# Adjacency loaded as 64 tiles of 4 MB into two buffers instead of 128 halves of 2 MB into four

## The chip, the core and the metric

The kernel runs on one core of a Trainium2 chip. The metric is the device time of one execution in microseconds (us). It works with five engines (TensorE for matmuls, VectorE, ScalarE, GpSimd, and SyncE, which only issues transfers) and with the core's 16 DMA engines. In the profile they are called PE (its weight loads PEld), DVE, ACT, POOL and SP.

## What is computed

One layer of graph attention over a sparse adjacency matrix. `x` is 8192 x 128 float32; `adj` is 8192 x 8192 int32, with a one in some 4 of the 8192 places of a row; `attn` is 256 x 1.

```python
h = jnp.maximum(_layernorm(x, axis=-1), 0.0)
s_i = h @ attn[:d]
s_j = h @ attn[d:]
e = jax.nn.leaky_relu(s_i + s_j.T, negative_slope=0.2)
e = e + jnp.where(adj > 0, jnp.float32(0.0), neg_inf)
alpha = jax.nn.softmax(e, axis=1)
return x + alpha @ h
```

The 256 MB of `adj` have to be read once; everything else is small beside them.

## The kernel before

**Tiles.** The 8192 rows are cut into 64 tiles of 128 rows (row `64 * p + t` stands in partition p of tile t). Two tiles are a pair. A tile of the adjacency is 128 partitions with 8192 int32 each, 32 KB in a row and 4 MB in all. The kernel handles it in two halves of 4096 columns; half n is half n % 2 of tile n // 2.

**The loads.** `adj_ring` holds four halves (64 KB in each partition). SP issues all loads, in `load_pair(p)`: the four halves of pair p, each as one transfer (line 356) of 2 MB, 16 KB from each of 128 rows, into slot `n % 4`. Each slot has its own semaphore `adj_in[s]`. The first four are issued at once. From then on the load of half n waits until half n - 4 has been signed (`signed`, line 355), so that up to four halves are under way or waiting to be used. After the loads of pair p, SP issues the store of pair p - 4 of the output (128 KB, line 361).

**The stages behind a load.** ACT turns a half into signs (`sign_tile`, line 533, int32 to bf16, with the row's sum as a by-product) and counts `signed`. PE packs the eight chunks of a tile's signs into one number per column (`pack_tile`, lines 1152 and 1160: four or eight matmuls as soon as a half is signed) and counts `packed`. DVE finds the columns with ones by maxima over these numbers (`max_tile`, `find_pair`, `flag_pair`, `key_pair`). POOL fetches the neighbours' rows of h by indirect DMA from a table in HBM (`gather_pair`, line 455, twelve gathers for a pair; rows of crowded lists by line 470). DVE scores them (`score_pair`), ACT takes the exponential (`exp_pair`, between the two halves of a pair's first tile), and DVE adds them up (`add_pair`, line 797).

**The start.** ACT's own order is fixed by hand: the layer norm of x by quarters (`root_quarter`, `relu_quarter`, line 544, 16 activations for a quarter) and, between them, `sign_tile(0)` behind `relu_quarter(1)` and `sign_tile(1)` behind `relu_quarter(2)`. The scored rows of h are stored to the table in four transfers of 1 MB, issued by POOL (line 441), and the first gather waits for all of them.

**The end.** When the last tile is through, DVE does the parts that need all rows (`lone_mark` and what follows), and the last lists and the last two pairs are mixed.

The order on every engine is the order of the code; no scheduler moves anything.

Of the kernel before, what the change touches and what calls it, by code (L numbers as in the profile page):

```python
# [5 lines left out]
def graph_attention_kernel(nc: bass.Bass, x: bass.AP, adj: bass.AP, attn: bass.AP, out: bass.AP):  # L6
# [10 lines left out]
    HALF = N // 2  # L17
# [52 lines left out]
    adj_t = adj.rearrange("(p t) c -> t p c", p=P)  # L70
# [3 lines left out]
    with ctx:  # L74
        def sb(name, shape, dt):
            return ctx.enter_context(nc.sbuf_tensor(name, shape, dt))
# [4 lines left out]
        def sem(name):  # L81
            return ctx.enter_context(nc.semaphore(name))

        adj_ring = sb("adj_ring", [P, 4, HALF], i32)
# [151 lines left out]

        x_in = [sem(f"x_in{i}") for i in range(XC)]
        attn_in = sem("attn_in")
        adj_in = [sem(f"adj_in{i}") for i in range(4)]
        consts = sem("consts")  # L240
        near_zeroed = sem("near_zeroed")
        ones_ready = sem("ones_ready")
# [17 lines left out]
        signed = sem("signed")  # L260
# [83 lines left out]
        @block.sync  # L344
        def _(sp):
            for c in range(XC):
                sp.dma_start(x_all[:, c * XT:(c + 1) * XT, :], x_t[:, c * XT:(c + 1) * XT, :]).then_inc(x_in[c], 16)
                if c == 0:
                    sp.dma_start(attn_b[:, :], attn.rearrange("d o -> o d").broadcast_to([P, 2 * D])) \
                        .then_inc(attn_in, 16)  # L350

            def load_pair(p):
                for s in range(4):
                    if p > 0:
                        sp.wait_ge(signed, 4 * p + s - 3)
                    sp.dma_start(adj_ring[:, s, :], adj_t[2 * p + s // 2, :, (s % 2) * HALF:(s % 2 + 1) * HALF]) \
                        .then_inc(adj_in[s], 16)

            def store_pair(g):
                sp.wait_ge(pair_mixed, g + 1)  # L360
                sp.dma_start(out_t[:, 2 * g:2 * g + 2, :], mixed[:, g % 2, :, :]).then_inc(stored[g % 2], 16)

            load_pair(0)
            load_pair(1)
            for p in range(2, PAIRS):
                load_pair(p)
                for g in MIXES.get(p - 2, []):
                    store_pair(g)
            for g in range(PAIRS - 4, PAIRS):
                store_pair(g)  # L370

            sp.wait_ge(sizes_ready, 2)
            tiles = sp.value_load(far_tiles[0:1, 0:1], min_val=1, max_val=TILES)
            parts = sp.value_load(far_parts[0:1, 0:1], min_val=1, max_val=DC)
            with sp.Fori(0, tiles) as t:
                with sp.Fori(0, parts) as c:
                    sp.wait_ge(far_used, DC * t + c + 1)
                    sp.sem_inc(sp_passed, 1)
                    sp.dma_start(far_h, table[ds(c * DW + 1, DW), :].rearrange("(k q) c -> q k c", q=P)) \
                        .then_inc(far_h_in, 16)  # L380
                    sp.dma_start(far_adj, adj_t[ds(t, 1), :, ds(c * DW, DW)].rearrange("o p w -> (o p) w")) \
                        .then_inc(far_adj_in, 16)
# [140 lines left out]
        @block.scalar  # L523
        def _(act):
            act.wait_ge(consts, 1)

            def sign_tile(t, halves=(0, 1)):
                for h in halves:
                    n = 2 * t + h
                    act.wait_ge(adj_in[n % 4], 16 * (n // 4) + 16)  # L530
                    if n >= 4:
                        act.wait_ge(packed, n - 3)
                    nc.scalar.activation(sign_ring[:, n % 4, :], adj_ring[:, n % 4, :], ACT.Sign, bias=half_neg[:, :],  # L533
                                         accum_out=degree[:, t, h:h + 1]).then_inc(signed, 1)

            def root_quarter(c):
                cs = slice(c * XT, (c + 1) * XT)
                act.wait_ge(setup, 8 * c + 8)
                nc.scalar.activation(rstd[:, cs], var[:, cs], ACT.Sqrt).then_inc(std_ready, 1)

            def relu_quarter(c):
                act.wait_ge(scaled, 2 * c + 2)
                for t in range(c * XT, (c + 1) * XT):
                    nc.scalar.activation(h_all[:, t, 0:D], x_all[:, t, :], ACT.Relu,  # L544
                                         bias=shift[:, t:t + 1], scale=rstd[:, t:t + 1]).then_inc(h_ready, 1)

            def exp_pair(g):
                act.wait_ge(below_ready, g + 1)
                nc.scalar.activation(weight[:, g % 2, :], below[:, g % 2, :], ACT.Exp).then_inc(weight_ready, 1)

            def exp_m(m):
                act.wait_ge(below_m_ready, m + 1)
                nc.scalar.activation(weight_m[:, :], below_m[:, :], ACT.Exp, accum_out=total_m[:, :]) \
                    .then_inc(weight_m_ready, 1)

            root_quarter(0)
            root_quarter(1)
            relu_quarter(0)
            root_quarter(2)
            root_quarter(3)  # L560
            relu_quarter(1)
            sign_tile(0)
            relu_quarter(2)
            sign_tile(1)
            def exp_step(p):
                for g in MIXES.get(p, []):
                    exp_pair(g)
                m = p // SEG - 1
                if m >= 0 and p % SEG == DEEP_MIX:
                    exp_m(m)  # L570

            for p in range(1, PAIRS):
                sign_tile(2 * p, (0,))
                exp_step(p - 1)
                sign_tile(2 * p, (1,))
                sign_tile(2 * p + 1)
            exp_step(PAIRS - 1)
            for c in range(LC):
                part = lone_p[:, c * LT * P:(c + 1) * LT * P]
                act.wait_ge(lone_masked, c + 1)  # L580
                nc.scalar.activation(part, part, ACT.Exp).then_inc(lone_exp, 1)  # L581
            exp_pair(PAIRS - 2)
            exp_pair(PAIRS - 1)
            exp_m(SEGS - 1)

            act.wait_ge(sizes_ready, 2)
            tiles = act.value_load(far_tiles[0:1, 0:1], min_val=1, max_val=TILES)
            parts = act.value_load(far_parts[0:1, 0:1], min_val=1, max_val=DC)
            with act.Fori(0, tiles) as t:
                with act.Fori(0, parts) as c:  # L590
                    act.wait_ge(far_neg_ready, DC * t + c + 1)
                    act.sem_inc(act_passed, 1)
                    nc.scalar.activation(far_p, far_masked, ACT.Exp, bias=far_neg[:, :]).then_inc(far_exp, 1)
                    nc.scalar.activation(far_scale[:, :], far_old[:, :], ACT.Exp, bias=far_neg[:, :]) \
                        .then_inc(far_exp, 1)
                    act.wait_ge(far_turned, DC * t + c + 1)
                    act.sem_inc(act_passed, 1)
                    nc.scalar.activation(far_pt, far_u, ACT.Copy).then_inc(far_pt_ready, 1)
# [687 lines left out]
```

## Time and profile before

| | us |
|---|---|
| median of 3 runs | 868.03 |
| lowest, highest | 866.7, 868.43 |
| the profiled execution, its own time | 867.93 |
| its span (first to last record) | 866.2 |

So 1.7 us of the profiled execution lie outside its span, and it is 0.1 us from the median. Busy times of the span: DVE 66%, POOL 66%, ACT 60%, PE 53%. "DMA share" is the mean busy share of the 16 DMA engines. A time in a view counts from the span's start. A wait in the views names what came last before the engine went on; a transfer's "to landing" is from its issue on SP or POOL to the semaphore that tells its end.

### The profile page before, as it was taken

How to read it: one execution, taken by the hardware profiler on the slowest of the kernel's cores; microseconds unless marked ns; L12 is line 12 of the kernel's file. 1: busy time of each engine (PE TensorE's matmuls, PEld its weight loads, DVE VectorE, ACT ScalarE, POOL GpSimd, SP SyncE). 2: the span in 40 equal slices, each digit the busy share in tenths (PEclk: the TensorE clock that was granted, in tenths of full speed). 3: DMA queues.
4: the chain of work that ended last, by engine and by line, in shares of the span. 5: the costliest groups of instructions: out<-in, count | busy, mean ns of one | idle time of the engine just before them, and what ended most of it. 6: DMA issues, size and time to landing. Idle time of an engine off the chain costs nothing.

```text
span 866.2 us, 7055 instructions
## 1 busy us (share of the span) xinstructions
PE 460.1 (53%) x1605; PEld 191.2 (22%) x1633; DVE 569.3 (66%) x2273; ACT 521.1 (60%) x357; POOL 571.0 (66%) x527
## 2 busy tenths in 40 slices
PE   0665465655555665566555656556566455623601
PEld 0332122221212222122222222222222122213600
DVE  7998266565676666656766465568656566668981
ACT  1895676666676666676666666667666677600200
POOL 6631776666567777666678777667776867758810
PEclk9998777676886678776788686876767788665955
DMA  8799999999999999999999999999999999511000
GB/s 346 286 382 404 399 406 409 410 410 410 406 408 409 410 408 409 405 410 411 404 406 410 408 411 406 414 405 412 404 405 403 408 391 404 196 25 27 18 16 14
DMA packets 39515, 301.56 MB, mean 348 GB/s; under 512 B 10611, under 2 KB 16948, under 8 KB 22065
## 3 DMA queue, kind: packets, MB, share of 16 engines
q1 hardware_dynamic: 24176, 277.23, 79.1%
q0 software_dynamic: 15296, 23.88, 8.0%
q8 instruction: 13, 0.21, 0.1%
q14 instruction: 30, 0.24, 0.1%
HBM read 303.63 MB, written 8.91 MB: 361 GB/s over the span
## 4 chain that ended last, share of the span: by engine, by line
DMA 69%; issue 13%; DVE 11%; ACT 5%; PE 1%; DVEq 0%; POOL 0%; SPq 0%; ACTq 0%; POOLq 0%
DMA adj_ring<-in_adj_dram 68%; ACT sign_ring L533 3%; DVE mixed L797 1%; DVE one_hot L609 1%; ACT h_all L544 1%; DVE adj_ring L954 1%; DVE adj_ring L958 1%; DVE adj_ring L949 1%; DVE mixed_m L879 1%; DMA x_all<-in_x_dram 1%; PE words L1160 0%; DVE codes L616 0%; DVE codes L619 0%; PE words L1220 0%; PE words L1223 0%
## 5 line engine op out<-in xcount | busy, mean ns | idle before, releaser
L533 ACT ACTIVATE sign_ring<-adj_ring,half_neg 128x4096 bf16<-128x4096 int32 x128 | 474.6, 3708 | 226.4 <-DMA adj_ring<-in_adj_dram 226.4
L455 POOL DMA_INDIRECT near<-h_table,near_id x384 | 443.8, 1156 | 198.9 <-issue 109.2
L1160 PE MATMUL words<-sign_ring,pack_w 128*128 128x512 bf16 x1004 | 357.2, 516 | 282.3 <-ACT sign_ring L533 279.6
L656 DVE MAX8 cand<-words 128x8 f32<-128x256 f32 x256 | 91.1, 418 | 223.9 <-PE words L1160 223.8
L1160 PEld LDWEIGHTS words<-sign_ring,pack_w 128*128 128x128 bf16 x1024 | 114.1, 121 | 516.7 <-ACT sign_ring L533 357.2
L797 DVE SCALAR_TENSOR_TENSOR mixed<-near,weight_n,mixed 128x128 f32<-128x128 f32 x448 | 120.3, 345 | 0.0
L470 POOL DMA_INDIRECT near_m<-h_table,id_m x64 | 79.1, 1235 | 19.5 <-issue 19.5
L1152 PE MATMUL words<-place,place_w 128*128 128x512 bf16 x120 | 47.2, 478 | 1.1 <-issue 1.0
L1142 PE MATMUL listing<-h_all 128*1 128x128 f32 x128 | 20.4, 335 | 33.7 <-ACT h_all L544 33.7
L581 ACT ACTIVATE adj_ring<-adj_ring 128x2048 f32<-128x2048 f32 x4 | 7.6, 1910 | 49.8 <-DVE adj_ring L958 49.8
L1179 PEld LDWEIGHTS listing<-cand,one_hot 128*128 128x128 f32 x128 | 28.1, 271 | 12.6 <-issue 6.5
L1229 PE MATMUL words<-h_all,adj_ring 128*128 128x129 f32 x128 | 18.8, 316 | 15.7 <-ACT adj_ring L581 15.7
L1179 PE MATMUL listing<-cand,one_hot 128*128 128x34 f32 x128 | 23.3, 317 | 2.5 <-DVE one_hot L745 2.5
L533 ACT ACTIVATION_READ_ACCUMULATOR sign_ring<-adj_ring,half_neg 128x1 f32 x128 | 23.9, 186 | 0.0
L434 POOL TENSOR_SCALAR h_all<-x_all,codes 128x128 f32<-128x128 f32 x16 | 13.0, 825 | 14.5 <-DVE codes L628 14.5
L1142 PEld LDWEIGHTS listing<-h_all 128*1 128x1 f32 x128 | 12.8, 102 | 41.4 <-issue 27.1
L672 DVE TENSOR_TENSOR codes<-cand_i,code_mask 128x512 int32<-128x512 int32 x32 | 21.9, 684 | 0.0
L1229 PEld LDWEIGHTS words<-h_all,adj_ring 128*128 128x128 f32 x128 | 18.1, 229 | 16.4 <-ACT adj_ring L581 16.4
L642 DVE TENSOR_TENSOR near<-h_all,mixed 128x2048 f32<-128x2048 f32 x8 | 21.5, 2683 | 0.0
L797 DVE SCALAR_TENSOR_TENSOR mixed<-near,weight_n,x_all 128x128 f32<-128x128 f32 x64 | 19.8, 350 | 1.1
L544 ACT ACTIVATE h_all<-x_all,codes 128x128 f32<-128x128 f32 x48 | 18.8, 480 | 0.2 <-DVE codes L628 0.2
L647 DVE TENSOR_REDUCE h_all<-near 128x16 f32<-128x2048 f32 x8 | 18.3, 2288 | 0.3
(213 smaller groups left out, 431.4 us busy)
## 6 DMA issues: line engine op xcount, KB each, us to landing
adj_ring<-in_adj_dram SPq DMA_DIRECT2D x128, 2048.0 KB, 18.9
near<-h_table,near_id POOLq DMA_INDIRECT x384, 6.4
h_table<-h_all POOLq DMA_DIRECT2D x4, 1056.0 KB, 12.2
x_all<-in_x_dram SPq DMA_DIRECT2D x4, 1024.0 KB, 9.6
out_dram<-mixed SPq DMA_DIRECT2D x32, 128.0 KB, 18.5
near_m<-h_table,id_m POOLq DMA_INDIRECT x64, 6.2
adj_ring<-h_table SPq DMA_DIRECT2D x1, 132.0 KB, 3.1
mixed<-in_L_gnn_attn_dram SPq DMA_DIRECT2D x1, 128.0 KB, 6.5
```

Of the source, the lines that this page charges most:

```text
L455: pool.indirect_dma_start(out=near[:, p % RING, k, :], out_offset=None, in_=table, in_offset=bass.IndirectOffsetOnAxis(ap=near_id[:, p % I ...
L470: pool.indirect_dma_start(out=near_m[:, k, :], out_offset=None, in_=table, in_offset=bass.IndirectOffsetOnAxis(ap=id_m[:, k:k + 1], axis=0 ...
L533: nc.scalar.activation(sign_ring[:, n % 4, :], adj_ring[:, n % 4, :], ACT.Sign, bias=half_neg[:, :], accum_out=degree[:, t, h:h + 1]).then ...
L544: nc.scalar.activation(h_all[:, t, 0:D], x_all[:, t, :], ACT.Relu, bias=shift[:, t:t + 1], scale=rstd[:, t:t + 1]).then_inc(h_ready, 1)
L656: last = nc.vector.max(out=cand[:, p % 2, t % 2, 8 * q:8 * q + 8], in_=words[t % 3][:, q * PART:(q + 1) * PART])
L672: nc.vector.tensor_tensor(codes[:, :, :, :].rearrange("p a w c -> p (a w) c"), cand_i[:, :, :].rearrange("p a w -> p (a w)").unsqueeze(2). ...
L797: ins = nc.vector.scalar_tensor_tensor(acc, near[:, e, slot, 0:D], weight_n[:, a * own + k:a * own + k + 1], base, ALU.mult, ALU.add)
L1142: last = nc.tensor.matmul(listing[0:1, 0:D], h_all[:, t, ONE:ONE + 1], h_all[:, t, 0:D], start=(t == 0), stop=(t == TILES - 1))
L1152: nc.tensor.matmul(at[:, k * BANK:(k + 1) * BANK], place_w[:, :], place[:, k * BANK:(k + 1) * BANK], start=True, stop=False)
L1160: last = nc.tensor.matmul(at[:, k * BANK:(k + 1) * BANK], pack_w[:, c, :], sign_ring[:, n % 4, o + k * BANK:o + (k + 1) * BANK], start=Fal ...
L1179: last = nc.tensor.matmul(listing[:, 0:REC], one_hot[:, p % 2, a, :], cand[:, p % 2, a, :], start=(p % SEG == 0 and a == 0), stop=(p % SEG ...
L1229: last = nc.tensor.matmul(lone_sum, lone_p[:, t * P:(t + 1) * P], h_all[:, t, 0:ONE + 1], start=(t == 0), stop=(t == TILES - 1))
```

## The change

A load brings a whole tile, in one transfer of 128 rows with 32 KB each, into two neighbouring slots. There are two semaphores, one for each half of the ring. The load of tile t waits until both halves of tile t - 2 have been signed. ACT waits for its tile's semaphore ahead of either half. The memory used, the signs, their ring of four halves and all else stay.

```diff
-        adj_in = [sem(f"adj_in{i}") for i in range(4)]
+        adj_in = [sem(f"adj_in{i}") for i in range(2)]
...
             def load_pair(p):
-                for s in range(4):
+                for e in range(2):
                     if p > 0:
-                        sp.wait_ge(signed, 4 * p + s - 3)
-                    sp.dma_start(adj_ring[:, s, :], adj_t[2 * p + s // 2, :, (s % 2) * HALF:(s % 2 + 1) * HALF]) \
-                        .then_inc(adj_in[s], 16)
+                        sp.wait_ge(signed, 4 * p + 2 * e - 2)
+                    sp.dma_start(adj_ring[:, 2 * e:2 * e + 2, :].rearrange("p h c -> p (h c)"), adj_t[2 * p + e, :, :]) \
+                        .then_inc(adj_in[e], 16)
...
                     n = 2 * t + h
-                    act.wait_ge(adj_in[n % 4], 16 * (n // 4) + 16)
+                    act.wait_ge(adj_in[t % 2], 16 * (t // 2) + 16)
```

On SP, from the loads of x to the second store, the order before is:

```order
L347 DMA x_all<-in_x_dram 128x2048 x3
L356 DMA adj_ring<-in_adj_dram 128x4096 x4
L356 DMA adj_ring<-in_adj_dram 128x4096 [waits signed] x16
L361 DMA out_dram<-mixed 128x256 [waits pair_mixed]
L356 DMA adj_ring<-in_adj_dram 128x4096 [waits signed] x4
L361 DMA out_dram<-mixed 128x256 [waits pair_mixed]
```

and now, at the same place:

```order
L347 DMA x_all<-in_x_dram 128x2048 x3
L356 DMA adj_ring<-in_adj_dram 128x8192 x2
L356 DMA adj_ring<-in_adj_dram 128x8192 [waits signed] x8
L361 DMA out_dram<-mixed 128x256 [waits pair_mixed]
L356 DMA adj_ring<-in_adj_dram 128x8192 [waits signed] x2
L361 DMA out_dram<-mixed 128x256 [waits pair_mixed]
```

Nothing has moved past another instruction; each two loads have become one of twice the width, and the stores stand between the same tiles. On ACT the place is the two signs of tile 0, the quarter of the layer norm behind them, and tile 1; each half waited for a semaphore of its own, and now both halves of a tile wait for the same one:

```order
-L533 ACTIVATE sign_ring,degree<-adj_ring,half_neg 128x4096 [waits adj_in0]
-L533 ACTIVATE sign_ring,degree<-adj_ring,half_neg 128x4096 [waits adj_in1]
+L533 ACTIVATE sign_ring,degree<-adj_ring,half_neg 128x4096 [waits adj_in0] x2
 L544 ACTIVATE h_all<-x_all,codes 128x128 [waits scaled]
 L544 ACTIVATE h_all<-x_all,codes 128x128 x15
-L533 ACTIVATE sign_ring,degree<-adj_ring,half_neg 128x4096 [waits adj_in2]
-L533 ACTIVATE sign_ring,degree<-adj_ring,half_neg 128x4096 [waits adj_in3]
```

The order of ACT's instructions is the same as before; only what they wait for differs. PE, DVE and POOL have the same instructions and waits.

## Rows read from the trace of the kernel before

**Rows 1.** Page, parts 1 and 2: busy time, share and instructions; DMA packets by size.

```profile
PE 460.1 (53%) x1605; PEld 191.2 (22%) x1633; DVE 569.3 (66%) x2273; ACT 521.1 (60%) x357; POOL 571.0 (66%) x527
...
DMA packets 39515, 301.56 MB, mean 348 GB/s; under 512 B 10611, under 2 KB 16948, under 8 KB 22065
```

**Rows 2.** Chain that ended last, in order of time: start us, us, what.

```profile
101.33 0.19 ACT sign_ring L533
101.54 18.81 DMA adj_ring<-in_adj_dram
120.40 3.59 issue
...
736.15 0.19 ACT sign_ring L533
```

**Rows 3.** Waits of the whole span: who for whom: us, times, longest.

```profile
PE words L1160 <- ACT sign_ring L533: 279.6, 118, 4.7
ACT sign_ring L533 <- DMA adj_ring<-in_adj_dram: 226.4, 122, 4.1
DVE cand L656 <- PE words L1160: 223.8, 46, 9.2
```

**Rows 4.** Busy time by stretch; the last three: PEclk, DMA share, GB/s.

```profile
10.00:20.00 10.00, 0.00 (x0) 0.00 (x0) 9.78 (x29) 1.52 (x3) 5.63 (x23) 1.00 1.02 431
...
36.00:41.00 5.00, 4.97 (x32) 3.18 (x32) 4.97 (x3) 5.00 (x3) 5.00 (x7) 0.70 0.11 29
41.00:52.00 11.00, 6.62 (x30) 3.08 (x31) 10.93 (x5) 11.00 (x19) 8.63 (x7) 0.87 0.99 380
52.00:66.00 14.00, 10.01 (x70) 5.84 (x68) 13.90 (x7) 13.64 (x9) 0.76 (x2) 0.98 0.99 375
66.00:88.00 22.00, 12.53 (x53) 5.52 (x55) 18.57 (x74) 12.37 (x7) 4.28 (x6) 0.84 0.99 407
...
110.00:736.00 626.00, 362.60 (x1138) 133.76 (x1159) 394.88 (x1765) 424.00 (x252) 445.25 (x388) 0.75 1.01 407
```

**Rows 5.** Timeline of ACT at the start: start us, us, what.

```profile
35.60 3.69 ACT L533 ACTIVATE sign_ring<-adj_ring,half_neg 128x4096 bf16<-128x4096 int32 x1
...
39.29 3.70 ACT L533 ACTIVATE sign_ring<-adj_ring,half_neg 128x4096 bf16<-128x4096 int32 x1
```

**Rows 6.** Tile adj_ring, 39.3 to 39.5 us: the load issued there.

```profile
L356 SPq DMA_DIRECT2D adj_ring<-in_adj_dram x1: 327/327/327, 39.4 to 39.4; - x1
...
DMA to landing us min/median/max: 8.0/8.0/8.0
```

**Rows 7.** DMA issues: transfer, queue, count, KB each, median us to landing.

```profile
adj_ring<-in_adj_dram SPq DMA_DIRECT2D x128, 2048.0 KB, 18.9
near<-h_table,near_id POOLq DMA_INDIRECT x384, 6.4
...
adj_ring<-h_table SPq DMA_DIRECT2D x1, 132.0 KB, 3.1
```

**Rows 8.** Timeline of ACT, 403 to 440 us: the second half of four tiles.

```profile
403.34 3.71 ACT L533 ACTIVATE sign_ring<-adj_ring,half_neg 128x4096 bf16<-128x4096 int32 x1 [1.60 <-DMA adj_ring<-in_adj_dram]
...
414.05 3.71 ACT L533 ACTIVATE sign_ring<-adj_ring,half_neg 128x4096 bf16<-128x4096 int32 x1 [1.46 <-DMA adj_ring<-in_adj_dram]
...
425.81 3.71 ACT L533 ACTIVATE sign_ring<-adj_ring,half_neg 128x4096 bf16<-128x4096 int32 x1 [1.77 <-DMA adj_ring<-in_adj_dram]
...
437.48 3.71 ACT L533 ACTIVATE sign_ring<-adj_ring,half_neg 128x4096 bf16<-128x4096 int32 x1 [2.86 <-DMA adj_ring<-in_adj_dram]
```

**Rows 9.** Page, part 3: DMA queues: packets, MB, share of 16 engines.

```profile
q1 hardware_dynamic: 24176, 277.23, 79.1%
q0 software_dynamic: 15296, 23.88, 8.0%
```

**Rows 10.** Chain that ended last, from the last load's issue on.

```profile
755.26 3.81 ACT sign_ring L533 x2
...
759.12 3.57 PE words L1160 x8
```

## Prediction

> **What bounds the kernel now.** I read the page's chain of waits first, because every engine is only 53 to 66% busy [rows 1], so busy time alone names no bound. The chain is loads of the adjacency for most of the span, and in order of time it is one pattern, repeated [rows 2]: ACT finishes a half, SP issues the next load into that slot, the load lands 18.8 us later, ACT signs (3.6 us as "issue" and 0.2 us), and so on. A turn of this pattern is four halves, one pair. Between its first and last piece shown there are 28 turns in 736.15 - 101.33 = 634.8 us, so a pair takes 22.67 us, a tile 11.34, a half 5.67. The table of waits says who is late in there: PE waits for ACT, DVE for PE, ACT for the loads, 122 times [rows 3]. ACT needs 3.9 us for a half and gets one every 5.67, so the compute side has room. The stretches say why the loads are late: from 110 to 736 us the DMA engines are busy all the time, at 407 GB/s [rows 4]. So the middle is bound by the DMA engines' work, not by the time from issue to landing. The 18.9 us of a load [rows 7] are mostly queueing: at its issue nearly three other halves (3 x 5.67 = 17 us) stand ahead of it.
>
> The question for the change is therefore not what a transfer costs, but whether the engines still always have work. A larger transfer in the same memory gives the same bytes, with a slot that comes free later and data that can be used later.
>
> **Part 1, the start: +3.7 us.** The ring is full before ACT is ready to sign: from 36 to 41 us the DMA engines are at 0.11 of their time [rows 4]. The first half is signed from 35.60 to 39.29 and the second to 42.99 [rows 5]. The fifth load is issued at 39.4 [rows 6]; its successor, the load of tile 2, must wait for both halves, to about 43.1. The hole grows by one sign, 3.7 us. What would hide this is a later hole in the same stretch, which could shrink. There is none: the shares of the stretches from 41 to 88 us are 0.98 to 0.99 [rows 4], work of loads and table stores together. Tile 3 is issued as its second half was before. So the whole stream moves by 3.7 us. Bounds: 0 (if a hole later on takes it up) and 3.7; I take 3.7, because the stretches show no such hole.
>
> **Part 2, the end: +3.7 us.** Of the last tile, the first half is already signed when the second lands. Then come one sign, 3.81 us with its accumulator read, and one group of 8 matmuls, 3.57 us [rows 10]. Afterwards the tile lands as a whole and ACT signs two halves, 2 x 3.7. PE packs the first of them beside the second sign, 3.57 us under 3.7, so only one sign more lies on the path. DVE waits for that and everything behind it moves. Bounds 3.6 and 3.9.
>
> **Part 3, the middle: +2.5 us, uncertain.** Here the depth decides. Let a tile land at T. Before, the slot of half n was free 3.8 us after landing, with three halves ahead of the new load. Now both halves are signed at T + 7.4, with 0.2 for the exponential in between on every other tile and 0.1 to the issue: T + 7.6 to 7.7. The only work left for the slowest DMA engine is tile t + 1, due to land at T + 11.34. For the stream not to pause, the fixed part of a load (issue to first byte, and last byte to semaphore) has to fit into 11.34 - 7.65 = 3.7 us. One load of the trace was issued into an empty queue and tells this part: 8.0 us from issue to landing [rows 6], of which 2.10 MB at the 431 GB/s of the stretch from 10 to 20 us are 4.9 us (an estimate; at the middle's 407 it would be 5.15) [rows 4], so 3.1 fixed. The 132 KB load at the end takes 3.1 in all [rows 7]. These two agree although one is 16 times larger, so I take 3.1 for 4 MB also. Room on average: 0.6 us.
>
> Tiles are not even, though. The starts of the second halves in the timeline are 10.7, 11.8 and 11.7 us apart [rows 8]. I carried this rule through the 56 tiles whose second halves start between 120.4 [rows 2] and 755.3 us [rows 10] (56 distances, mean 11.34): each tile takes its own distance on the stream, and starts when the one ahead is through or 3.1 us less the landing part after its issue, whichever is later. The pauses add up to 2.5 us with 3.1 fixed, 0.1 with 2.6, 5 with 3.3, 10 with 3.6, 22 with 4.2 and 41 with 4.9. I take 2.5.
>
> In the trace the gathers, which are tiny, land 6.4 us after issue [rows 7] under full load, twice the 3.1 of the lone small load. Part of that is POOL's own issuing and part waiting behind load packets, but some can be slower access under load, which a fixed part read from an idle machine does not have. The Trainium skill, "DMA: Bandwidth & Descriptors", section on latency and other measured facts, speaks against this change here: HBM access takes 0.2 us on average and 2 us at high load, and it is the main component of the fixed cost. By that rule up to 1.8 us would come on top; the rows neither show nor exclude it.
>
> **Part 4, fewer packets: -3.2 us.** A row of 16 KB is one packet now: 128 x 128 = 16384 of the 24176 packets of q1 [rows 9], near the 39515 - 22065 = 17450 packets of 8 KB and more [rows 1]. With 32 KB rows there are 8192 fewer, if the queue does not split them. What does a packet cost beside its bytes? Two queues give two equations [rows 9]. q1 took 0.791 x 16 x 866.2 = 10963 us of engine time for 24176 packets and 277.23 MB; q0 took 0.080 x 16 x 866.2 = 1109 us for 15296 packets and 23.88 MB. Solved, a packet costs 12.5 ns. 8192 x 12.5 ns / 16 engines = 6.4 us. The packets of the two queues are of different kinds, so this is a rough estimate; 0 (rows split back, or no such cost) and 6.4 are the bounds, and I take the middle, since neither queue has only such packets.
>
> **What is free.** SP issues 64 instructions fewer, 0.33 us each [rows 6], in time it spends waiting. `signed`, `packed` and the ring of signs are untouched; a sign in the second tile on needs a half packed four halves ago, 22.67 us of stream earlier. PE gets its halves in bursts of two, 2 x 4 us of matmuls in 11.34. The exponential's input comes from DVE one pair ahead. Table stores share the engines with packets twice as long, so they may end some us later; DVE then gets its first gathers later, but ACT needs what PE packed four halves earlier, so the stages behind ACT can slip by some us without reaching a load. If this cover were gone, the start would cost those few us more.
>
> **Sum.** 867.93 (the profiled execution's own time) + 3.7 + 3.7 + 2.5 - 3.2 = 874.6. The profiled execution is 0.1 from the median 868.03, so the median of after should be **874.7**, 0.8% slower.
>
> **Rivals.**
>
> *A. The queue runs dry for every tile.* Same mechanism as part 3, but the fixed part of a 4 MB load issued under load is 3.6 to 4.9 us. For it: the 6.4 us of the gathers, and the rule above. Against it: 2 MB and 132 KB have the same fixed part. It decides from about 3.3 us on. Time: 872.2 (the sum without its 2.5) + 10 to 41 = 882 to 913; with 4.2, 894. Signs: ACT's wait for the load would start to follow SP's issue, and the DMA share of the middle would fall to 0.97 or less.
>
> *B. No change.* The ends cost 7.4, packets give the full 6.4, and the fixed part is near 2.6: 867.93 + 7.4 + 0.1 - 6.4 = 869.0. For it: the equations of part 4. Against it: all three must fall its way.
>
> *C. Faster.* The stream has room: it moves 407 GB/s in the middle while the stretch from 10 to 20 us reached 431 [rows 4]. If longer packets alone raised the rate by 2%, 0.02 x 635 = 12.7 us, the time would be 867.93 + 7.4 + 2.5 - 12.7 = 865.1. It decides from 10 us of gain on, a rate 1.6% higher. The Trainium skill, same page, section on bandwidth, has a rule that would give more: 341 GB/s for 1 MB transfers and 425 for 16 MB. This holds for transfers measured one by one; the rows of the middle show no idle time between transfers for a larger one to remove. Against C: the bytes and the engines' time for a byte are unchanged, and the gathers take their share as before.
>
> *D. The rows are split into 16 KB again.* Then part 4 is zero: 877.8, inside the forecast's own range.
>
> **How the numbers follow.** Forecast (with D) 0.58, from 870 to 881: ends 7.4, middle 0 to 8, packets 0 to -6.4. A 0.25, from 881 to 913. B 0.12, C 0.05. A measurement here can tell about 0.2%, 1.7 us: below 866.3 is faster, up to 869.8 the same. That gives faster 0.05, same 0.12, slower 0.83. The range of 868.5 to 894 leaves out C, a little of B, and the upper part of A.
>
> **What would show it.** The fifth load's counterpart issued near 43 us and a hole in the DMA share some 3.7 us longer: part 1. Two signs and one pack behind the last landing: part 2. The distance of tiles in the middle: 11.34 plus 0.04 for part 3, less 0.06 for part 4; over 11.5 would be A, under 11.2 C. q1 with about 16,000 packets instead of 24,176 would show the longer rows. The prediction is wrong above all if the fixed part of a large load under load is not 3.1 us.

## The result, and the profile after

The changed kernel takes 887.8 us (median of 4 runs, 884.3 to 890.2) against 867.4 beside it. The ratio is 1.023 with a 95% interval of 1.019 to 1.027, so it is 2.3% slower. The profiled execution took 889.62 us with a span of 887.9, that is 21.7 more than the profiled one before. The ratios below leave out executions more than 1.5% above the fastest of their kernel (one of 1858 us, of the kernel with halves first, among them), and the traces of the kernel with the first scoring later and of the one freed by halves and used by tiles are of such executions, so their waits, rates and delays at a tile are read and not their totals.

I predicted 874.7 and gave 868.5 to 894: the sign was right and the size was inside the range, but the loss of 20.4 us is three times the 6.7 I called likeliest. The surprise is where the time went. First the page's parts 1 to 3 and 6, to compare with [rows 1], [rows 7] and [rows 9]:

```profile
span 887.9 us, 6991 instructions
...
DMA packets 30298, 301.56 MB, mean 340 GB/s; under 512 B 9586, under 2 KB 15923, under 8 KB 21040
...
q1 hardware_dynamic: 14960, 277.23, 78.0%
q0 software_dynamic: 15296, 23.88, 8.2%
...
adj_ring<-in_adj_dram SPq DMA_DIRECT2D x64, 4096.0 KB, 15.1
...
h_table<-h_all POOLq DMA_DIRECT2D x4, 1056.0 KB, 24.5
```

The rows of 32 KB travel as one packet each: q1 has 9216 packets fewer, the 8192 of the rows and 1024 that belong to the 64 transfers saved. The 1 MB stores of the table, which the change doesn't touch, land after 24.5 us (median); before:

```profile
h_table<-h_all POOLq DMA_DIRECT2D x4, 1056.0 KB, 12.2
```

The stretches of after (the last three columns are PEclk, DMA share, GB/s), to compare with [rows 4]:

```profile
36.00:41.00 5.00, 5.00 (x32) 3.08 (x31) 4.96 (x3) 5.00 (x3) 5.00 (x7) 0.66 0.00 0
41.00:52.00 11.00, 6.61 (x35) 3.38 (x36) 10.93 (x5) 11.00 (x19) 8.63 (x7) 0.92 0.68 268
...
110.00:736.00 626.00, 344.16 (x1116) 124.26 (x1137) 387.07 (x1723) 410.58 (x250) 446.71 (x392) 0.76 0.99 395
...
118.00:128.00 10.00, 0.00 (x0) 0.00 (x0) 1.22 (x8) 2.01 (x3) 7.80 (x8) 0.52 0.74 288
128.00:136.00 8.00, 7.12 (x27) 3.23 (x29) 7.35 (x36) 7.97 (x6) 6.14 (x7) 0.74 0.50 146
```

The first hole is longer, as expected: (1 - 0.68) x 11 + 5 = 8.5 us against 0.89 x 5 + 0.01 x 11 = 4.6 before, so 3.9. But there is a second one between 118 and 136 us that I had not forecast: 0.26 x 10 + 0.50 x 8 = 6.6 us of the DMA engines' time. The chain of waits of after shows its cause, in order of time:

```profile
70.34 32.29 DMA h_table<-mixed
...
118.07 8.55 DMA near<-h_table,near_id
...
126.64 0.23 DVE score L753
...
128.03 0.02 ACT weight L549
```

Loads are no longer on the chain there. The last store of the table lands after 32 us, the twelve gathers of pair 0 can start only then, DVE waits for them to score pair 0, and ACT waits for DVE to take the exponential between the two signs of tile 6. The two traces' tables of waits, after and then before:

```profile
POOL near L455 <- DMA h_table<-mixed: 32.7, 1, 32.7
DVE score L753 <- DMA near<-h_table,near_id: 27.8, 5, 22.5
...
ACT weight L549 <- DVE below L769: 18.4, 3, 8.0
```

```profile
POOL near L455 <- DMA h_table<-mixed: 13.0, 1, 13.0
```

ACT's timeline at tile 6, before and after. The table load in it is for the exponential's function:

```profile
107.30 1.28 ACT L549 ACT_TABLE_LOAD   x1
108.59 0.22 ACT L549 ACTIVATE weight<-below 128x16 f32<-128x16 f32 x1
109.16 3.71 ACT L533 ACTIVATE sign_ring<-adj_ring,half_neg 128x4096 bf16<-128x4096 int32 x1 [0.35 <-DMA adj_ring<-in_adj_dram]
...
131.74 3.71 ACT L533 ACTIVATE sign_ring<-adj_ring,half_neg 128x4096 bf16<-128x4096 int32 x1 [1.63 <-DMA adj_ring<-in_adj_dram]
```

```profile
114.92 3.71 ACT L533 ACTIVATE sign_ring<-adj_ring,half_neg 128x4096 bf16<-128x4096 int32 x1 [3.50 <-DMA adj_ring<-in_adj_dram]
...
118.74 1.28 ACT L549 ACT_TABLE_LOAD   x1
128.03 0.21 ACT L549 ACTIVATE weight<-below 128x16 f32<-128x16 f32 x1 [8.00 <-DVE below L769]
128.15 3.69 ACT L533 ACTIVATE sign_ring<-adj_ring,half_neg 128x4096 bf16<-128x4096 int32 x1
...
146.04 3.71 ACT L533 ACTIVATE sign_ring<-adj_ring,half_neg 128x4096 bf16<-128x4096 int32 x1 [6.71 <-DMA adj_ring<-in_adj_dram]
```

A tile is complete when its second half starts before the change and its first half after it. That gives the account of the 21.7 us:

| | before | after | late by |
|---|---|---|---|
| tile 6 complete | 109.16 | 114.92 | 5.8 |
| tile 8 complete | 131.74 | 146.04 | 14.3 |
| tile 63 complete | 755.26 | 775.32 | 20.1 |
| end of span | 866.2 | 887.9 | 21.7 |

So 14.3 us are lost in the first 146 us, of which 8.5 between tiles 6 and 8 (of the 5.8 up to tile 6, the longer hole explains 3.9; the rest was not traced), 5.8 us in the 55 tiles of the middle, and 1.6 behind the last landing.

### The profile page after: what moved, and what is told of

It is laid out like the page before. It is cut to its first block, busy times and chain, and to the rows that moved or that the text cites. A ratio compares the mean times of both kernels' runs of the same rounds, so it can differ in the third digit from the quotient of the medians.

```text
span 887.9 us, 6991 instructions
## 1 busy us (share of the span) xinstructions
PE 446.1 (50%) x1605; PEld 182.5 (21%) x1633; DVE 570.9 (64%) x2273; ACT 514.5 (58%) x357; POOL 567.6 (64%) x527
## 3 DMA queue, kind: packets, MB, share of 16 engines
q1 hardware_dynamic: 14960, 277.23, 78.0%
## 4 chain that ended last, share of the span: by engine, by line
DMA 54%; issue 15%; DVE 14%; ACT 13%; POOL 1%; PE 1%; DVEq 0%; SPq 0%; ACTq 0%; POOLq 0%
DMA adj_ring<-in_adj_dram 49%; ACT sign_ring L533 13%; DMA h_table<-mixed 4%; DVE near L642 2%; DVE mixed L797 1%; DVE one_hot L609 1%; POOL near L455 1%; DVE adj_ring L954 1%; DVE adj_ring L958 1%; DVE adj_ring L949 1%; DMA near<-h_table,near_id 1%; DVE mixed_m L879 1%; DVE h_all L647 1%; DMA x_all<-in_x_dram 1%; DVE codes L616 0%
## 5 line engine op out<-in xcount | busy, mean ns | idle before, releaser
L1152 PE MATMUL words<-place,place_w 128*128 128x512 bf16 x120 | 37.7, 390 | 0.9 <-issue 0.7
L1179 PE MATMUL listing<-cand,one_hot 128*128 128x34 f32 x128 | 19.9, 284 | 19.2 <-DVE one_hot L745 19.2
L1179 PEld LDWEIGHTS listing<-cand,one_hot 128*128 128x128 f32 x128 | 22.3, 221 | 25.6 <-DVE one_hot L745 20.3
L753 DVE TENSOR_SCALAR score<-near,h_all 128x8 f32<-128x8 f32 x32 | 7.6, 237 | 28.0 <-DMA near<-h_table,near_id 27.8
## 6 DMA issues: line engine op xcount, KB each, us to landing
adj_ring<-in_adj_dram SPq DMA_DIRECT2D x64, 4096.0 KB, 15.1
h_table<-h_all POOLq DMA_DIRECT2D x4, 1056.0 KB, 24.5
out_dram<-mixed SPq DMA_DIRECT2D x32, 128.0 KB
mixed<-in_L_gnn_attn_dram SPq DMA_DIRECT2D x1, 128.0 KB, 6.3
```

The lines of the kernel that those rows point to most:

```text
L1152: nc.tensor.matmul(at[:, k * BANK:(k + 1) * BANK], place_w[:, :], place[:, k * BANK:(k + 1) * BANK], start=True, stop=False)
L1179: last = nc.tensor.matmul(listing[:, 0:REC], one_hot[:, p % 2, a, :], cand[:, p % 2, a, :], start=(p % SEG == 0 and a == 0), stop=(p % SEG ...
```

## Experiments

The kernel before took 882 and 880 us (medians) in the two sessions of the first eight runs and 866 in that of the last four. So only ratios to the kernel before of the same session are compared between sessions, and traces by stretches. Starts at tile 0 differ by 2.8 us in some traces; delays at a tile are taken from ACT's first sign.

The kernel before was not traced in the first two sessions, and their traces differ from the others in two ways that don't follow the form of the loads. Behind 330 us the rate falls even in kernels with a fine ring, as the lines further down show. And from the last tile's completion to the end of the span they take 110 to 128 us, where the traces of the other sessions take 110 to 113. So the stretch from 160 to 330 us is what I compare, and a difference of some us between two totals of these sessions is not put down to a stage.

**Whole tiles by two transfers: are the long packets the cause?**

```diff
-                    sp.dma_start(adj_ring[:, 2 * e:2 * e + 2, :].rearrange("p h c -> p (h c)"), adj_t[2 * p + e, :, :]) \
-                        .then_inc(adj_in[e], 16)
+                    for h in range(2):
+                        sp.dma_start(adj_ring[:, 2 * e + h, :], adj_t[2 * p + e, :, h * HALF:(h + 1) * HALF]) \
+                            .then_inc(adj_in[e], 16)
...
-                    act.wait_ge(adj_in[t % 2], 16 * (t // 2) + 16)
+                    act.wait_ge(adj_in[t % 2], 32 * (t // 2) + 32)
```

> The changed kernel, but each tile comes by two transfers of 2 MB (16 KB rows) that are issued together once the whole tile is free; ACT still waits for the whole tile. Only the length of a packet differs from the changed kernel. Theory P (32 KB packets take the DMA engines from the table's stores, whose packets are 8 KB; the table is late by 20 us, DVE waits 22.5 us for the first gather, ACT 8 us for its exponential): the last part of the table lands 13 to 15 us after its issue instead of 32.3, DVE's wait for the gathers is near 12, no stall of ACT, and the time is 887.8 - 8 = 877 to 880. Theory D (the late table comes from the stream as a whole being late or from the slots that free late, not from the packets): table wait and time stay as in the changed kernel, 886 to 890.

Measured: 1.028 (1.021 to 1.035) times before. Its table of waits and two stretches, the second around the issue of a tile's two loads at 201 us:

```profile
POOL near L456 <- DMA h_table<-mixed: 14.1, 1, 14.1
```

```profile
160.00:330.00 170.00, 90.07 (x288) 31.81 (x294) 99.38 (x447) 107.43 (x64) 102.57 (x96) 0.74 1.00 383
```

```profile
202.00:204.00 2.00, 1.95 (x11) 1.04 (x10) 0.68 (x2) 0.00 (x0) 0.00 (x0) 1.00 0.85 279
```

With 16 KB rows the table is on time again (14.1 us instead of 32.7), ACT is held up 1.5 us at tile 6 instead of 9.5, and tile 8 is 5.0 us late instead of 14.3. Theory P holds for the start. Its time was a miss: the total did not fall, because the middle is slower here, 383 GB/s between 160 and 330 us. From tile 8 to tile 63 this kernel loses 28 us, where the changed kernel loses 5.8. Neither theory had that. I come back to it below.

**The first scoring one pair later: does ACT's stall cost what it lasts?**

```diff
-        MIXES = {p: [p - 2] for p in range(2, PAIRS)}
+        MIXES = {p: [p - 2] if p > 3 else [0, 1] for p in range(3, PAIRS)}
```

> The changed kernel with the first pair scored one pair later (pairs 0 and 1 are both mixed in turn 3), so that DVE doesn't wait for the first gather in turn 2. Loads and packets as in the changed kernel. Theory P and D both say that the table stays late (32 us). If the stall of ACT behind DVE's wait is what costs (tile 8 starts 14.3 us late, tile 6 only 5.8), the time falls by about 8 to 879 to 881. If that stall would have been made up later by the stream, the time stays at 886 to 890.

Measured: 1.023 (1.013 to 1.033). The table stayed late (POOL waited 30.5 us). Tile 8 was now only 3.7 us late, about what the first hole gives, so what the changed kernel loses beyond it up to tile 8 hangs on the stall. But the stall had only moved: ACT waited at tile 8, for the exponential of pair 1. POOL issues a gather every 1.3 us, so 24 gathers for two pairs take 31 us from 102 us on, and one pair's respite is too little:

```profile
139.51 1.28 ACT L549 ACT_TABLE_LOAD   x1
140.81 0.21 ACT L549 ACTIVATE weight<-below 128x16 f32<-128x16 f32 x1
148.22 0.22 ACT L549 ACTIVATE weight<-below 128x16 f32<-128x16 f32 x1 [7.20 <-issue]
```

My expected 8 us of gain was a miss; the experiment shows the mechanism up to tile 8, not a remedy. Its executions scatter widely, from 892.6 to 906.3 us.

**Halves at the start, tiles later, and the reverse: how much belongs to which stretch?** `load_pair` and `sign_tile` follow the old form for some pairs and the new one for the rest, with semaphores of their own:

```diff
+                    if p < 5:       # the reverse kernel: p >= 5
+                        for h in range(2):
+                            if p > 0:
+                                sp.wait_ge(signed, 4 * p + 2 * e + h - 3)
+                            sp.dma_start(adj_ring[:, 2 * e + h, :], adj_t[2 * p + e, :, h * HALF:(h + 1) * HALF]) \
+                                .then_inc(half_in[2 * e + h], 16)
+                        continue
...
```

> Pairs 0 to 4 by halves as before the change, pairs 5 to 31 by whole tiles. If the start holds most of the loss, as the two traces say (14.3 of 21.7 us by tile 8, 5.7 from there to tile 63, 1.6 behind), the time is that of before + 6 to 9: 873 to 877. If the loss lies in every tile of the middle (fixed part of a load above 3.6 us), it is 884 to 890.

> The other way round: pairs 0 to 4 by whole tiles, the rest by halves. If the start holds most of the loss: before + 13 to 15, 880 to 883. If the middle holds it: 869 to 872 (only the 3.7 of the start).

Measured: 1.012 (1.002 to 1.022) with halves first, 1.022 (1.016 to 1.028) with tiles first. In the traces, tile 8 is 0.0 us late with halves first and 13.1 with tiles first. From 160 to 330 us the first moves 399 GB/s and the second 409, what the kernel before has. So the loss up to tile 8 belongs to the way the first pairs are loaded (row length and grain together), and the lower rate from 160 to 330 us to the way the later ones are. The time with halves first lies in its expected range (6 to 9 us is 0.7 to 1.0%); that with tiles first, 2.2%, is above the 13 to 15 us expected, and its stretches behind 330 us move only 398 and 391 GB/s, although they are loaded by halves. The two losses add to more than the changed kernel's, but the intervals are wide.

**The changed kernel again, in the same session.**

> The changed kernel once more, beside the experiments on the same chip, since the kernel before ran at 882 us in the chip session of the first experiments and at 867 beside the first runs. Both theories: 1.8 to 2.8% over the kernel before; the table's last part lands 30 us or more after its issue.

Measured: 1.018 (1.013 to 1.024); POOL waited 30.6 us for the table.

**Which coarseness costs in the middle: freeing or using?** One kernel frees by tiles and uses by halves (the load's wait before the halves 0 and 2 of a pair only); the other frees by halves and uses by tiles.

```diff
-                    if p > 0:
-                        sp.wait_ge(signed, 4 * p + s - 3)
+                    if p > 0 and s % 2 == 0:
+                        sp.wait_ge(signed, 4 * p + s - 2)
```

> Transfers of 2 MB with 16 KB rows, issued in twos once a whole tile is free, but ACT signs a half as soon as that half lands. Theory G (in the middle the cost comes from the coarse grain: slot free 7.6 us after the tile lands): signing begins 5 us before the tile is complete, so the slots free some 3.7 us earlier than in the changed kernel, the queue never dries, and the middle is as before; with the start's 3.7 us the time is that of before + 3 to 5 us (0.4 to 0.6%). Theory Q (two loads issued together cost something of their own, as in the kernel of two loads for a tile, which was no faster than the changed one): 2% or more over before.

```diff
-                    act.wait_ge(adj_in[n % 4], 16 * (n // 4) + 16)
+                    for both in (2 * t, 2 * t + 1):
+                        act.wait_ge(adj_in[both % 4], 16 * (both // 4) + 16)
```

> Loads exactly as before the change, each issued when its half slot is free, but ACT waits for both halves of a tile. A slot frees 5.67 us later for the first half, 0 to 3.7 later for the second. Theory G: the load of the first half of tile t + 2 is issued at T + 3.8 with 7.5 us of stream ahead of it, so the middle stays as before; the start too, since ACT is the later there; the end costs one sign. Time: before + 3 to 5 us. If grain of use alone were the cost: 1.5% or more over before.

Measured: 1.011 (1.005 to 1.016) and 1.002 (0.998 to 1.006). The stretches of the two, in this order:

```profile
160.00:330.00 170.00, 100.04 (x314) 36.33 (x314) 105.43 (x471) 114.82 (x68) 112.75 (x99) 0.75 1.01 410
...
330.00:500.00 170.00, 102.26 (x308) 36.73 (x308) 105.26 (x467) 111.50 (x68) 117.69 (x104) 0.71 1.00 392
500.00:736.00 236.00, 135.85 (x428) 49.59 (x428) 152.16 (x669) 158.69 (x97) 161.94 (x146) 0.71 1.00 398
```

```profile
160.00:330.00 170.00, 99.28 (x317) 35.33 (x316) 104.54 (x465) 113.59 (x68) 113.96 (x102) 0.75 1.01 409
...
330.00:500.00 170.00, 98.83 (x313) 35.06 (x311) 107.89 (x481) 110.22 (x68) 117.11 (x104) 0.74 1.00 398
500.00:736.00 236.00, 126.60 (x434) 46.54 (x435) 144.94 (x636) 156.51 (x97) 154.63 (x141) 0.77 0.99 393
```

and the first of them in the changed kernel:

```profile
160.00:330.00 170.00, 97.71 (x309) 35.06 (x316) 102.67 (x461) 112.24 (x68) 114.31 (x102) 0.75 1.00 404
```

Between 160 and 330 us either coarseness alone keeps the rate of before, 409 GB/s; both together have 383 with 16 KB rows and 401 to 404 with 32 KB rows. The times agree for 16 KB rows: 1.028 with both, 1.011 and 1.002 with one. So theory G holds there. It is weaker than that in two ways. Behind 330 us these two kernels move 392 to 398 GB/s, no more than the changed kernel in the same session (400 and 401), while the kernel before, traced in another session, moved 408 and 405; whether that is the session or the ring no run here shows. And the loss of rate does not appear in the DMA share, which is 1.00 in all these stretches; that the queue runs low is read from the two microseconds at 202 us alone. A tile that is freed whole costs 3.9 us at tile 8 in the trace, which is the first hole alone; its 1.1% in the time are more than the 0.4 to 0.6 expected, though the interval reaches down to 0.5.

**Half the depth: how long is the fixed part of a load under load?**

```diff
-                    if p > 0:
-                        sp.wait_ge(signed, 4 * p + s - 3)
+                    if p > 0 or s > 1:
+                        sp.wait_ge(signed, 4 * p + s - 1)
```

> The kernel before, but a half's load waits until half n - 2 is signed: two halves of 2 MB in flight or in use instead of four. It measures the fixed part F of a load under load. A half's turn is then landing, 3.8 us sign and issue, F, and 5.67 us of data for two halves of the stream: a half takes (3.8 + F + 5.67) / 2 if that is over 5.67. With F = 3.1, as read from the load into the empty queue: 6.29 us a half, 128 x 0.62 = 79 us more than before. With F = 1.9 or less: no difference. With F = 4.9 (slower under load): 7.2 us, 195 us more.

Measured, by two executions: 998.8 us against 866.1, 1.154 (1.149 to 1.160), so 132.7 us or 1.04 us for each of 128 halves. A half takes 5.67 + 1.04 = 6.71, and by the rule of the expectation F = 2 x 6.71 - 3.8 - 5.67 = 3.95 us, an estimate. Its landings and its middle:

```profile
DMA to landing us min/median/max: 8.3/9.4/11.4
```

```profile
110.00:736.00 626.00, 347.69 (x973) 123.83 (x991) 336.83 (x1500) 363.87 (x219) 367.41 (x321) 0.67 0.93 344
```

So by this rule F is 3.95 under load, not 3.1. Measured directly, a load takes 9.4 us from issue to landing here against 8.0 into the empty queue. The Trainium skill, "DMA: Bandwidth & Descriptors", latency and other measured facts, has 0.2 us on average and 2 us at high load for an access to HBM, up to 1.8 more. The 0.85 worked out here lie within it. Part of the 0.85 is no latency: the engines are idle for only 0.07 x 6.71 = 0.5 of the 1.04 us lost in a half, and per unit of busy time they move less, 344 / 0.93 = 370 GB/s here against 407 / 1.01 = 403 before [rows 4].

**Wider stores of the table: does the share go by packets?**

```diff
-            for c in range(XC):
+            for c in range(1, XC, 2):
                 pool.wait_ge(scores_ready, 2 * c + 2)
-                pool.dma_start(table_t[:, c * XT:(c + 1) * XT, :], h_all[:, c * XT:(c + 1) * XT, :]) \
+                pool.dma_start(table_t[:, (c - 1) * XT:(c + 1) * XT, :], h_all[:, (c - 1) * XT:(c + 1) * XT, :]) \
...
-            pool.wait_ge(table_out, 16 * (XC + 1))
+            pool.wait_ge(table_out, 16 * (XC // 2 + 1))
```

> The changed kernel, its table stored by two transfers of 2 MB instead of four of 1 MB, so that a store's packets are 16.9 KB instead of 8.4 and have to wait behind half as many 32 KB packets. Theory P (engines shared by packets in turn): the table's last part lands after 17 to 23 us instead of 30 to 32, POOL waits that long, ACT's stall of 8 us behind the first exponential shrinks to 0 to 2, and the time falls by 6 to 9 us against the changed kernel (to 1.0 to 1.2% over the kernel before in a session that gave the changed kernel 1.8%). If long packets harm the table otherwise (by bytes, or by slower writes): wait and time unchanged.

Measured: 1.021 (1.015 to 1.027). POOL waited 22.8 us for the table, not 30.6 to 32.7, although the third quarter now starts 9 us later than it could:

```profile
POOL near L455 <- DMA h_table<-mixed: 22.8, 1, 22.8
DVE score L753 <- DMA near<-h_table,near_id: 22.3, 3, 20.4
```

ACT waited 5.7 us for the exponential instead of 8.0, and tile 8 was 10.9 us late instead of 14.3. The direction is theory P's and the wait is in its range; the gain at tile 8 is half of what I expected, because 20 us of DVE's wait remain, and in the times (1.021, where 1.010 to 1.012 was expected) it can't be told from none. The Trainium skill has the rule on the same page, in queues, rings and completion order: an engine takes turns between its queues packet by packet. The traces agree in the direction, not in the size: the same 1 MB store takes 12.2 us beside 16 KB packets and 22.0 to 24.5 beside 32 KB ones, 1.8 to 2.0 times as long, where turns alone would make it 1.65 times.

**Shorter packets than before.** Each half by two transfers of 1 MB, issued together:

```diff
+                    for q in range(2):
+                        at = (s % 2) * HALF + q * HALF // 2
+                        sp.dma_start(adj_ring[:, s, q * HALF // 2:(q + 1) * HALF // 2],
+                                     adj_t[2 * p + s // 2, :, at:at + HALF // 2]).then_inc(adj_in[s], 16)
...
-                    act.wait_ge(adj_in[n % 4], 16 * (n // 4) + 16)
+                    act.wait_ge(adj_in[n % 4], 32 * (n // 4) + 32)
```

> The kernel before with each half brought by two transfers of 1 MB (8 KB rows), issued together. Theory P (share by packets): against 8 KB packets the table's stores, 8.4 KB too, get a larger share and the last part lands in less than the 12.5 us of before, 9 to 11, POOL's wait for the table under 11 us. The time stays within 0.5% of before since the table wasn't on the path there; 16384 packets more at 7 to 12 ns and 16 engines could add 7 to 13 us, if packets have the price that my prediction worked out from the queues' shares. If they have none: 0 to 2 us.

Measured: 1109 us, 1.261 (1.255 to 1.267). A plain miss of both of its expectations: 229 us more than the 879.9 beside it instead of 0 to 13, and POOL waited 13.1 us for the table, no less than before. By turns little was to be seen: 8.4 of 16.6 KB at 301 GB/s leave a store 152 GB/s, 8.4 of 24.8 KB at 407 leave it 138 (estimates). So this run speaks neither for theory P nor against it.

```profile
q1 hardware_dynamic: 42608, 277.24, 83.0%
```

```profile
110.00:736.00 626.00, 318.50 (x862) 109.27 (x861) 284.74 (x1268) 315.38 (x187) 313.81 (x280) 0.63 1.00 301
```

The engines are fully busy at 301 GB/s, so they run out of nothing: the work itself takes them longer. Whether that is the shorter row or the order in which two transfers at once ask for their rows was not separated. q1's engine time is 0.830 x 16 x 1109.5 = 14734 us against 10963 before [rows 9], 3771 more for 18432 packets more, 205 ns each on average.

**A better start for the kernel before.** ACT signs tile 0 earlier; a second kernel adds the later first scoring.

```diff
             root_quarter(2)
+            sign_tile(0, (0,))
             root_quarter(3)
             relu_quarter(1)
-            sign_tile(0)
+            sign_tile(0, (1,))
```

> The kernel before with the two signs of tile 0 earlier in ACT's order: the first half after root_quarter(2), in 2.6 us in which ACT waits for DVE, the second behind relu_quarter(1). It attacks the hole of the DMA engines from 36.7 to 41 us, which the change made 3.7 us longer. If a hole there moves the whole stream, the fifth load is issued near 30 us, the hole goes, the seventh and eighth loads are issued about 1.3 us later, and the time falls by 2 to 4 us (0.2 to 0.5%). If the stream is bound later by something else (the first exponential, the first gathers): no difference.

> As the kernel with the early sign, with the first pair scored one pair later, so that ACT's first exponential (2 us ahead of its need in the kernel before) can't stop the earlier stream. If that exponential binds, this one is 1 to 3 us faster than the early sign alone; if not, the same.

Measured: 1.001 (0.999 to 1.003) and 1.000 (0.998 to 1.002), no difference. The hole moved rather than closed:

```profile
36.00:41.00 5.00, 4.31 (x21) 2.61 (x22) 4.97 (x3) 5.00 (x6) 5.00 (x7) 0.50 0.75 320
41.00:52.00 11.00, 10.68 (x69) 6.14 (x70) 10.93 (x4) 11.00 (x18) 9.21 (x6) 0.96 0.65 235
```

Its hole is 0.25 x 5 + 0.35 x 11 = 5.1 us, against 4.6 before: the first half comes sooner, but the loads behind it have to wait for the other signs, which are only some 3 us earlier. No kernel tried is faster than the one before beyond the interval.

## Why the prediction was right and wrong

**The bound: right.** The middle is the DMA engines' work, and the kernels whose ring is fine in one way or the other move 409 or 410 GB/s from 160 to 330 us, in every session.

**Part 1, the first hole, +3.7: right.** The hole grew by 3.9 us of engine time, and tile 8 is 3.9 us late in the kernel that frees by tiles with 16 KB rows and 5.0 in that which also uses by tiles.

**What I called free: the step that failed.** I wrote that the table's stores may end "some us later", that the stages behind ACT can slip, and that without this cover the start "would cost those few us more". The stores' last landing went from 12.5 to 32.3 us after issue, and the cover did not hold. I had looked for a limit at the ring of packed halves, and there is none; the limit was ACT's own instruction between two signs, which stops the signs whatever the rings hold. With only two tiles in the ring, this stop emptied the queue. Price: 9.3 us at tile 8 (14.3 late, against 5.0 with 16 KB rows). How much cover there was can be read from when DVE has the exponential's input ready. Before:

```profile
106.65 0.17 DVE L769 TENSOR_TENSOR below<-leaky,top 128x16 f32<-128x16 f32 x1
```

There the exponential began 1.8 us after its input was ready, because its table load stood in front, and ended 0.35 us before the load of tile 6's second half landed: 2.1 us of cover. In the changed kernel ACT itself comes to it later: the table load ends at 120.0, so the input could have come 13.2 us later than before without making ACT wait. It came at 128.0, 21.2 us later, and ACT waited 8.0. I could have named this path, but the turns of two row lengths do not give its price: a store has 8.4 of 24.8 KB before and 8.4 of 41 after, 1.65 times as long, which makes the last landing some 8 us later (an estimate) and no stall at all. It was 19.8 us later. Why the stores lost more than their turns stays open.

That the delay of tile 8 is still there at the end is what the trace of after shows (it stays at 14 to 16 us up to tile 31); the total times of the kernels without the stall don't show it by themselves, since each of them lost or scattered elsewhere.

**Part 3, the middle, +2.5: too small, and the 3.95 does not explain it.** With two halves of 2 MB ahead F comes out at 3.95 and not 3.1, which I had read from a load into an idle machine. But my own list gives 10 to 22 us for 3.6 to 4.2, and the trace has +5.8 for the whole middle, packets included; between the same tiles the changed kernel lost 4.9 us when it ran again and 2.3 with the wider table stores. A 4 MB load lands 15.1 us after issue in the median, and a stream that never pauses gives 2 x 11.34 - 7.65 = 15.0. So the rule fits the 4 MB loads with an F near 3.1 to 3.4. With 16 KB rows the coarse ring costs far more, 383 against 409 GB/s and 28 us in the middle, more than the rule gives for any F up to 4.2.

**Part 4, fewer packets, -3.2: wrong.** q1's engine time did not fall by 6.4 us an engine but rose, from 0.791 x 866.2 = 685 to 0.780 x 887.9 = 693 us. A packet has no fixed price: two queues with two different kinds of packets can't be solved for one. From 8 to 16 KB rows the difference is 205 ns a packet, from 16 to 32 KB no gain shows while the queue is full. Where the ring is coarse, 32 KB rows do better than 16 KB ones (401 to 404 against 383 GB/s from 160 to 330 us). I did not settle why: two transfers instead of one put the second half's issue 0.4 us later, and gathers that the long packets held back fill some of the gaps; neither was measured by itself.

**Part 2, the end, +3.7: half right.** The second sign is there, but the total behind the last landing is 1.6. Chain of after, against [rows 10]:

```profile
778.93 3.89 ACT sign_ring L533 x3
782.87 1.92 PE words L1160 x8
```

PE's last eight matmuls take 1.92 us instead of 3.57. The stretches show why, before and then after:

```profile
759.00:763.00 4.00, 3.88 (x12) 1.81 (x12) 0.29 (x1) 0.36 (x4) 2.69 (x3) 0.57 0.21 45
```

```profile
782.80:784.80 2.00, 1.93 (x11) 1.08 (x11) 0.00 (x0) 0.32 (x4) 0.00 (x0) 1.00 0.11 20
```

The granted clock is 1.00 (2.4 GHz) after and 0.57 before, mostly the lower level of 1.2 GHz. After the change PE had packed the tile's first half just ahead, beside the second sign; before, it had been waiting for ACT. This gives back 1.65 of the 3.9 us; the 0.6 between the 2.2 left and the 1.6 measured was not traced.

**The rivals.** The measured time lies outside the 870 to 881 of the forecast proper and in A's 882 to 913, but A would have had its whole loss in the middle, and two thirds of the loss are at the start. So that the stated range holds the result is luck: it was widened for a mechanism that cost 5.8 us at most. B and C are out. D is refuted by q1's 14960 packets. The sum as it came: 14.3 + 5.8 + 1.6 = 21.7, where I had 3.7, -0.7 and 3.7.

## What to carry to other kernels

When a bulk stream's transfers change their row length, look at the small transfers that share the DMA engines first, and then at who waits for them: here untouched stores took twice as long, and the stall behind them cost 9.3 of the 21.7 us. In this case a ring of fixed memory was freed coarsely at 1.1% and used coarsely at 0.2%, but both together cost 2.8% with the same rows, since they leave only the time of one load for everything between landing and the next first byte. And where an in-order engine feeds the ring, look for the instruction on it that waits for a long way round. Its slack is counted from when its input is ready to when it is needed, in the changed kernel and not in the old one: here 2.1 us before and 13.2 after, against a delay of 21.2.

## What the runs showed of the hardware

- 8 KB rows of a 2 MB pitch (row p of a tile starts 64 rows of 32 KB behind row p - 1) loaded at 301 GB/s with the engines fully busy, 16 KB rows at 391 to 410 in the middle of the kernels with a fine ring (403 to 410 in the sessions where the kernel before took 866 and 867 us), 32 KB rows no faster. I had expected 7 to 13 us of difference from 16 to 8 KB and it was 229.
- A 2 MB load took 8.0 us from issue to landing into an empty queue and 9.4 (median) in a ring of two. Less the data, the fixed part is worked out at 3.1 us in the one case and 3.95 in the other, an estimate.
- In the one stretch looked at, engines that restart after a pause moved less for their busy time: 279 GB/s at a share of 0.85 in the two microseconds behind an issue, 328 for a full share, against 403 in the full stream.
